# Expert outputs weighed and added in pieces of 128 rows, in a one-core language-model layer

## The reference

```
h = emb[tokens] * sqrt(256) + pos_enc            # 256 wide
h = softmax(q k^T / 16, over queries) v          # q, k, v = h w_q, h w_k, h w_v
h = h + mixer(layernorm(h))                      # projection, causal convolution over 4 steps,
                                                 # state-space scan in chunks of 128, gate, norm, projection
# mixture of 8 experts, two per token, 1024 slots each
scores = softmax(layernorm(h) @ w_router);  weights, experts = top_k(scores, 2)
slot   = expert * 1024 + position of this choice among the expert's choices
y      = gelu(x[slots of e] @ w1[e]) @ w2[e]     # 256 -> 1024 -> 256, for each expert e
out    = h + sum over a token's two experts of weight * y + bias
```

## Time and profile before

| | us |
|---|---|
| median of 3 runs (957.86 to 961.7) | 959.34 |
| the profiled execution, its own time | 958.16 |
| its span | 956.4 |
| mean granted TensorE clock | 0.965 of full speed |
| PE busy | 887.6 (93% of the span) |
| DVE, ACT, POOL busy | 631.6, 529.1, 505.9 |
| batches: from the start to the last scatter | about 559 |
| experts: from there to the end | about 397 |

### The profile page before, as it was taken

One profiled execution on the slowest core, in us unless ns is written; L12 is line 12 of the kernel. 1 busy time (PEld: TensorE's weight loads), 2 busy tenths in 40 slices (PEclk: granted clock), 3 DMA queues, 4 the chain that ended last, 5 costly groups with the idle time before them and its releaser, 6 DMA issues.

```text
span 956.4 us, 17255 instructions
## 1 busy us (share of the span) xinstructions
PE 887.6 (93%) x5580; PEld 785.6 (82%) x5580; DVE 631.6 (66%) x1662; ACT 529.1 (55%) x1094; POOL 505.9 (53%) x503
## 2 busy tenths in 40 slices
PE   5799999999999999999998539999999999999994
PEld 3688888888888888888886429999999999999993
DVE  2477899888988898889887344646363636363631
ACT  1466776677667767776766134545444544444430
POOL 6257776787678767877788311232333232323342
PEclk8799999999999999999998759999999999999998
DMA  8900011001000000000000034343343433332120
GB/s 269 330 26 12 34 46 33 22 33 33 12 22 13 23 13 23 20 16 14 21 22 26 14 103 132 90 88 105 67 109 72 109 72 104 72 105 28 23 61 34
DMA packets 48653, 58.62 MB, mean 61 GB/s; under 512 B 6336, under 2 KB 43819, under 8 KB 48624
## 3 DMA queue, kind: packets, MB, share of 16 engines
q1 hardware_dynamic: 33552, 41.05, 13.1%
q0 software_dynamic: 13632, 17.02, 10.6%
q10 hardware_dynamic: 1440, 0.17, 0.1%
HBM read 34.14 MB, written 29.75 MB: 67 GB/s over the span
## 4 chain that ended last, share of the span: by engine, by line
PE 81%; DVE 10%; issue 3%; POOL 2%; DMA 2%; ACT 1%; DVEq 0%; POOLq 0%; SPq 0%
PE bank L1592 13%; PE bank L1593 13%; PE bank L1594 13%; PE bank L1387 11%; PE bank L1497 5%; PE bank L1332 4%; PE bank L1477 4%; PE bank L1371 3%; PE bank L1346 3%; PE bank L1362 3%; PE bank L1353 3%; PE bank L1449 2%; DVE seg L1051 2%; PE bank L1512 2%; PE bank L1604 2%
## 5 line engine op out<-in xcount | busy, mean ns | idle before, releaser
L637 POOL DMA_INDIRECT out<-ye,tok_slot x56 | 96.7, 1727 | 254.3 <-DMA out<-ye,tok_slot 138.0
L877 ACT ACTIVATE hf<-bank 128x512 f32<-128x512 f32 x128 | 79.5, 621 | 202.4 <-PE bank L1594 201.1
L1264 DVE TENSOR_TENSOR h_lo<-hf,h_hi 128x512 fp32r<-128x512 f32 x128 | 88.6, 693 | 99.9 <-ACT h_hi L879 99.9
L1592 PE MATMUL bank<-w_hi,h_hi 128*128 128x256 f32 x512 | 146.2, 286 | 0.0
L1593 PE MATMUL bank<-w_lo,h_hi 128*128 128x256 f32 x512 | 144.9, 283 | 0.0
L1594 PE MATMUL bank<-w_hi,h_lo 128*128 128x256 f32 x512 | 144.9, 283 | 0.0
L1023 DVE SCALAR_TENSOR_TENSOR xc<-bank,cw,xc 128x253 f32<-128x253 f32 (+2 forms) x288 | 128.2, 469 | 1.7
L1592 PE MATMUL bank<-xe_hi,w_hi 128*128 128x512 f32 x256 | 100.8, 394 | 2.7 <-DVE xe_lo L1256 2.7
L1593 PE MATMUL bank<-xe_lo,w_hi 128*128 128x512 f32 x256 | 100.4, 392 | 0.0
L1594 PE MATMUL bank<-xe_hi,w_lo 128*128 128x512 f32 x256 | 100.2, 391 | 0.0
L585 POOL DMA_INDIRECT slots_dram<-rows,slot x64 | 63.4, 991 | 67.8 <-DVE slot L1152 53.2
(11 more groups left out here) (203 smaller groups left out, 2311.2 us busy)
## 6 DMA issues: line engine op xcount, KB each, us to landing
w_raw<-w SPq DMA_DIRECT2D x16, 1024.0 KB
slots_dram<-zero_row SPq DMA_DIRECT2D x1, 8320.0 KB, 29.7
xe<-slots_dram SPq DMA_DIRECT2D x16, 520.0 KB, 4.4
out<-hb SPq DMA_DIRECT2D x16, 256.0 KB, 2.1
w_raw<-in_wT SPq DMA_DIRECT2D x1, 1288.0 KB, 9.1
slots_dram<-rows,slot POOLq DMA_INDIRECT x64
out<-ye,tok_slot POOLq DMA_INDIRECT x64, 3.7
xg<-emb,idx POOLq DMA_INDIRECT x36, 4.1
```

The source lines that it names most:

```text
L637: g.indirect_dma_start(out, bass.IndirectOffsetOnAxis(ap=tok_slot[q][:, j:j + 1], axis=0), ye[q][:, j, :], None, compute_op=ALU.add).then_ ...
L877: sc.activation(hf[m % 2][:, :], h_bank[i % H_BANKS][:, :], ACT.Gelu_apprx_tanh)\
L1264: vc.tensor_tensor(h_lo[:, m, :], hf[m % 2][:, :], h_hi[:, m, :].bitcast(F32), ALU.subtract)\
L1592: te.matmul(out_, hi, rhi, start=first_, stop=False)
```

## The change

Three edits that have nothing to do with each other.

1. `second_product` alternates its four products between the two banks, one product of 128x256 in a bank at a time (`y_bank[j % 2]`), and waits on `ye_ready` before each. DVE weighs each product by itself (`tensor_scalar`, 128x256), and signals each; POOL waits for each piece. `low_weights` stays ahead of the first and the third weighing. The last group uses the same two banks; `last_product`, `weigh_onto` and `LAST_BANKS` go. Of the last expert only pieces 4 to 7 are fetched into `base` and written plainly; pieces 0 to 3 are added with accumulation as for other experts, after POOL has waited for the four fetches.
2. In the drain step that has b but no f, `gated_root` stands ahead of `scatter_rows`. In all other steps the order is as before.
3. SP waits for `w_q` and `w_k` to land before it issues `w_v`, `w_in` and `w_out`.

```diff
+            sp.wait_ge(s_qk, 32)
             sp.dma_start(wv[:, :, :], w_v.rearrange("(k p) n -> p k n", p=P)).then_inc(s_early, 16)
...
                 if t:
                     describe_rows(t, p)
+                if b and not f:
+                    gated_root(b, q)
+                if t:
                     scatter_rows(t, p)
-                if b:
+                if b and f:
                     gated_root(b, q)
...
             def fetch_sums():
 
-                for j in range(JS):
-                    g.indirect_dma_start(base[:, j, :], None, out,
+                for j in range(JS // 2, JS):
+                    g.indirect_dma_start(base[:, j - JS // 2, :], None, out,
...
+                pool.wait_ge(fetched, 16 * (JS // 2))
 
             def write_sums():
 
-                for j in range(JS):
+                for j in range(JS // 2):
+                    add_rows(NE, 1, j)
+                for j in range(JS // 2, JS):
...
                 def weigh(g):
                     q, half = g // NG, g % NG
-                    for b in range(2):
-                        if half == NG - 1 and not (last and q):
-                            low_weights(r * 2 + q, 1 - q, b, (w1_split, w2_split)[b])
-                        j = 4 * half + 2 * b
-                        dve.wait_ge(y_psum, r * (4 * NG) + (Y0 + 2 * g + b + 1 - 4 * NG))
-                        vc.tensor_tensor(ye[q][:, j:j + 2, :], y_bank[b][:, :].rearrange("p (j d) -> p j d", j=2),
...
+                    for n in range(4):
+                        if half == NG - 1 and n % 2 == 0 and not (last and q):
+                            low_weights(r * 2 + q, 1 - q, n // 2, (w1_split, w2_split)[n // 2])
+                        j = 4 * half + n
...
+                        dve.wait_ge(y_psum, r * (2 * JS) + (Y0 + 4 * g + n + 1 - 2 * JS))
...
+                            ins = vc.tensor_scalar(ye[q][:, j, :], y_bank[n % 2][:, 0:DM], w_slot[q][:, j:j + 1], None,
+                                                   ALU.mult)
+                        ins.then_inc(ye_ready, 1)
...
                 def second_product(g):
-                    q = g // NG
-                    pe.wait_ge(w2_split, r * 2 + (q - 1))
-                    for b in range(2):
-                        pe.wait_ge(ye_ready, r * (4 * NG) + (2 * g + b + 1 - 4 * NG))
-                        for j in (2 * b, 2 * b + 1):
-                            dst = y_bank[b][:, (j % 2) * DM:(j % 2 + 1) * DM]
...
+                    q = g // NG
+                    pe.wait_ge(w2_split, r * 2 + (q - 1))
                     for j in range(4):
...
+                        pe.wait_ge(ye_ready, r * (2 * JS) + (4 * g + j + 1 - 2 * JS))
```

More of the change, by code:

```diff
@@ L272, in lm_block @@
         ye = [eb(f"ye{q}", [P, JS, DM]) for q in range(2)]
-        base = eb("base", [P, JS, DM])
+        base = eb("base", [P, JS // 2, DM])
         e_now = eb("e_now", [P, 1])
@@ L360, in lm_block @@
         expert_added = sem("expert_added")
-        H_BANKS, Y0, CHUNKS = 4, 4 * NG, KF
+        H_BANKS, Y0, CHUNKS = 4, 2 * JS, KF
         CHUNK = 2 * KD * FF // CHUNKS
@@ L1265, in split_h @@
                             .then_inc(hlo_ready, 1)
-                def weigh_onto(g):
-                    half = g % NG
-                    if half == 0:
-                        dve.wait_ge(fetched, 16 * JS)
-                    for j in range(4 * half, 4 * half + 4):
-                        if half == 0:
-                            row, at = y_bank[j // 2], (j % 2) * DM
-                            dve.wait_ge(y_psum, Y0 + 4 * NG * (NE // 2 - 1) + 2 * g + j // 2 + 1)
-                        else:
-                            row, at = LAST_BANKS[j - 4], 0
-                            dve.wait_ge(y_psum, Y0 + 4 * NG * (NE // 2 - 1) + 2 * g + j - 4 + 1)
-                        ins = vc.scalar_tensor_tensor(out=ye[1][:, j, :], in0=row[:, at:at + DM],
-                                                      scalar=w_slot[1][:, j:j + 1], in1=base[:, j, :],
-                                                      op0=ALU.mult, op1=ALU.add)
-                        if half or j % 2:
-                            ins.then_inc(ye_ready, 1)
@@ L1285, in weigh @@
                 def weigh(g):
                     q, half = g // NG, g % NG
-                    for b in range(2):
-                        if half == NG - 1 and not (last and q):
-                            low_weights(r * 2 + q, 1 - q, b, (w1_split, w2_split)[b])
-                        j = 4 * half + 2 * b
-                        dve.wait_ge(y_psum, r * (4 * NG) + (Y0 + 2 * g + b + 1 - 4 * NG))
-                        vc.tensor_tensor(ye[q][:, j:j + 2, :], y_bank[b][:, :].rearrange("p (j d) -> p j d", j=2),
-                                         bc(w_slot[q][:, j:j + 2].unsqueeze(2), [P, 2, DM]), ALU.mult)\
-                            .then_inc(ye_ready, 1)
+                    for n in range(4):
+                        if half == NG - 1 and n % 2 == 0 and not (last and q):
+                            low_weights(r * 2 + q, 1 - q, n // 2, (w1_split, w2_split)[n // 2])
+                        j = 4 * half + n
+                        if last and g == 2 * NG - 1 and n == 0:
+                            dve.wait_ge(fetched, 16 * (JS // 2))
+                        dve.wait_ge(y_psum, r * (2 * JS) + (Y0 + 4 * g + n + 1 - 2 * JS))
+                        if last and g == 2 * NG - 1:
+                            ins = vc.scalar_tensor_tensor(out=ye[q][:, j, :], in0=y_bank[n % 2][:, 0:DM],
+                                                          scalar=w_slot[q][:, j:j + 1], in1=base[:, n, :],
+                                                          op0=ALU.mult, op1=ALU.add)
+                        else:
+                            ins = vc.tensor_scalar(ye[q][:, j, :], y_bank[n % 2][:, 0:DM], w_slot[q][:, j:j + 1], None,
+                                                   ALU.mult)
+                        ins.then_inc(ye_ready, 1)
@@ L1304, in experts @@
                         split_x(g + 1)
-                    if last and g >= NG:
-                        weigh_onto(g)
-                    else:
-                        weigh(g)
+                    weigh(g)
                     if g + 1 == NG:
@@ L1629, in last_product @@
                             at = slice(m * DM, (m + 1) * DM)
[L1630 to L1631 removed]
+                            ins = three(y_bank[j % 2][:, 0:DM], h_hi[:, m, j * P:(j + 1) * P],
+                                        h_lo[:, m, j * P:(j + 1) * P], w_hi[q][:, 1, at], w_lo[q][:, 1, at],
                                         m == 0, m == KF - 1)
[L1633 to L1647 removed]
                         ins.then_inc(y_psum, 1)
@@ L1656, in experts @@
                         turn_x(g + 1)
-                    if last and g + 1 == 2 * NG:
-                        last_product(g)
-                    else:
-                        second_product(g)
+                    second_product(g)
             experts(1, None)
```

28 lines of the change are left out of this document (8 added, 20 removed).

## The result

The changed kernel takes 968.93 us (median of 4 runs, 967.17 to 971.28); the kernel before took 958.6 beside it (4 runs, 957.26 to 961.7). The ratio is 1.0109, with a 95% interval of 1.0081 to 1.0137: some 10.3 us slower. The forecast was 963.8 with a range of 960.5 to 967.5. The direction was right, and the size was half of what came; the time lies above the range. The profiled execution is the one of 971.28, with a span of 969.5 us.

A forecast was written before the change was run, and what follows sets the result against it. PE was taken as the bound, with 81% of the chain. Stalls 8.4, end -0.75, drain +0.3 and start -2.7 gave +5.25 on 958.16, or 963.4; forecast 963.8, between that and the runs' median, range 960.5 to 967.5.

The forecast's parts named there:

- The stalls: Experts' groups with a weight split: PE waits 1.4 us for product 0's weighing, 7 times; 6 shift POOL's end, +8.4 us.
- Edit 2, +0.3: Drain step: the root runs earlier, but the later scatters delay the second root L558; +0.3 us, bounds -0.15 and +0.7.
- Edit 3, -2.7: Start: 2 MB of loads no longer compete with PE's two gathers; -2.7 us, bounds -3.3 and -1.2.
- Rival (a): Start: edit 3 gives nothing because late w_v or w_in makes POOL or DVE the wait; 966.1 us, chance 0.12.
- The estimate of 2.3 us: Start: a 128 KB gather would take 2.3 us by the skill's fit, so edit 3 would bring 3.5; outside the sum.
- The end, -0.75: POOL's last stretch: holds, fewer fetches, shorter wait and adds for writes sum to -0.75 us, bounds -1.8 and +0.5.
- the four adds: Last expert's end on POOL: four adds replace four writes, 18.6 us for 13.97, +4.6.
- from the first fetch to the first add: Last expert's end on POOL: four fetches instead of eight, -5.0 us, and a shorter wait behind the last fetch, -1.1.
- the holds and the later split: POOL before the last fetches: own holds for pieces 5 and 7 and a later weight split, +0.75 us, from none to 1.
- rival (c): Experts: the TensorE clock falls in the stalls, one slow product each, 17.3 us more; 980.7 us, chance 0.04.

The follow-up runs named there:

- edit 1 alone: Kernel before with only the 128-row products and weighings and the last expert's first half added: 968.55 us, ratio 1.0106.
- gathers_first: Kernel before, with the loads of in_wT and out_wT waiting until the first two gathers have landed, w_v issued as before: 960.6 us, ratio 1.0003.
- edit 3 alone: Kernel before with only SP's wait for the query and key weights ahead of the value weights and the loads behind them: 960.45 us, ratio 1.0016.
- the new end alone: Kernel before with only the last expert's end changed to four fetches, four adds and four writes: 958.16 us, ratio 0.9986.
- late splits: Changed kernel, all three edits, with the two weight splits moved behind the weighings of products 0 and 2: 957.07 us, ratio 0.9981.
- both splits ahead: Changed kernel with both weight splits ahead of the first weighing: 993.6 us, one run.
- bias_late: Changed kernel with the small load bias_b issued only once the first two gathers have landed: 968.68 us, one run.
- edit 2: As a run: kernel before with only the gated root moved ahead of the scatters in the drain step: 959.95 us, ratio 1.0010.
- late splits in the kernel before: Kernel before, banks of two products, with only the two weight splits moved behind the weighing of their bank: 960.41 us, ratio 1.0012.
- edit 1 with late splits: Kernel before with edit 1 and the two weight splits behind the weighings of products 0 and 2, no other edit: 956.0 us, ratio 0.9964.

## Why the forecast was half right

By its own steps:

- **The stalls, 7 waits and 6 in POOL's frame, 8.4 us: right in mechanism, place, number and size.** 1.45 each for a forecast of 1.4, and 8.48 in POOL's frame in the changed kernel, 8.13 in edit 1 alone. Moving the split away took them away, and doubling it ahead of the weighing gave 3.4 for 1.2. The weighing took 0.48 us and not 0.41, inside its bounds. No stall in the groups without a split: right.
- **Edit 2, +0.3: right.** L558 is released by a scatter, and the gain of the earlier root is taken back: -0.08 in the trace, +0.3 by the medians, neither to be told from nothing.
- **Edit 3, -2.7 (bounds -3.3 and -1.2): this is the step that failed**, in the sentence "2 MB of loads no longer compete with the two gathers that PE waits for". They do compete: the wait ends at 5.19, the gather was issued at 5.47 and needs about 4 us to land, as the 3.9 from its issue to PE's start in `gathers_first` and the median of 4.1 say, so the loads flow again before it has its bytes, and from 8 to 10 us not one byte of it moves in the changed kernel (in the profile of edit 3 alone the gathers' queue moved 0.04 MB there). Edit 3 alone cost 1.4 us in place of giving 2.7, a miss of 4.1 us, most of the 5.1 between forecast and result. Rival (a) was nearest (966.1), but it stopped at a gain of nothing. The estimate of 2.3 us that the forecast worked out beside the sum, by the fit in the Trainium skill (DMA: Bandwidth & Descriptors, Anatomy of one DMA — SWDGE (gpsimd) path), was of the same kind: it priced a gather with the engines to itself, and the shortest landing in the earlier trace rows is 3.4. That a gather takes its turn beside the loads, packet by packet (the Trainium skill, DMA: Bandwidth & Descriptors, Queues, rings and completion order), isn't what the changed kernel's trace shows from 8 to 10 us, where the gathers' queue has no packet at all and the two others have 320; why, no run shows. I had priced what a load removed gives, where the change only delays it; the gain was there for the taking only when the loads waited for the gathers' landing, and then POOL bounded it to 1.0.
- **The end, -0.75 (bounds -1.8 and +0.5): too low.** It was +0.89 in the changed kernel, +0.33 in edit 1 alone, +0.22 with the new end alone. The mis-sized term is the four adds: 18.6 forecast, from one add cycle of 4.71; they took 20.24, 19.79 and 19.87, since one of the four cycles is 5.4 to 6.0 us long; why wasn't found. The other terms were right: from the first fetch to the first add 7.43 in place of 13.37, -5.9 for a forecast of -6.1, and the holds and the later split ahead of the fetches 20.34 in place of 19.85, +0.5 for a forecast of +0.75. Of that 0.39 is the longer hold of the add of piece 4 under the weight split (3.21 for 2.82, last section).
- **The clock, rival (c): rightly set aside**, for a stall of this length.

The sum with what was measured: 8.5 + 0.3 to 0.9 + 0 + 1.4 = 10.2 to 10.8, for 10.3 by the medians. The 1.4 of edit 3 is the loosest of these terms: its interval runs from 0.1 to 2.9 us.

**What stays open.** In the profiles the experts' first product starts between 567.80 and 572.16. Set against the first root (L522 at the start), the fourteen starts sort themselves. In twelve profiles the experts start 540.1 to 540.8 us behind that root, whatever the edits; their whole spread was there at the start, where the root runs at 27.10 to 30.59. Only the changed kernel (544.44) and `gathers_first` (543.73) have some 3.5 us more, and these are the two in which the granted clock stays at 0.50 from 526 us to 538 and later; in the others it is back by 532 at the latest. `gathers_first` was 1.68 us ahead of the kernel before at its last root of the loop (489.92 against 491.60) and 1.96 behind at the experts' start. The 3.6 us of the drain in the changed kernel's profiled execution are no fixed price of its edits: the versions with late splits and with both splits ahead and `bias_late` have the same drain code and stand at 540.10, 540.55 and 540.23. What decides when the clock comes back was not found.

## What to carry to other kernels

When buffers are halved, look at what stands ahead of their reader on its engine: a piece of work that was hidden beside the second half of the old buffer lies on the path once the writer waits for the first half. Put it behind the short instruction that frees the buffer, and the smaller pieces gain (here -3.65 us in place of +9.5). And a load that is delayed isn't a load that is removed: ask whether it is still held when the transfer that it disturbs needs its bytes, and who waits for the delayed load next.

## What the runs showed of the hardware

- **How long a standstill costs the clock.** Behind the 7 stalls of 1.20 us in the changed kernel, and the 14 in edit 1 alone and `bias_late`, the granted clock stayed at 1.00. Of 7 stalls of 3.41 us it fell to 0.50 at six, at a price of 1.4 to 2.7 us each, which is up to 80% of the stall again. At the start, a wait of 3.46 us for the gather is followed by eight matmuls in 3.75, and a wait of 0.42 us by the same eight in 1.96.
- **The length of the slow stretch isn't the kernel's.** With one and the same code at the start, the second group of eight matmuls there took 1.99 us in four profiles (before, edit 1, edit 2, late splits in the kernel before) and 3.78 in two (the new end, edit 1 with late splits), 1.8 us of difference. The Trainium skill (TensorE: Matmul & The Clock Gate, What's actually happening) says that the number of slow matmuls at a start varies from run to run of one kernel; the traces agree. A comparison of single executions is blind to 2 us for this alone, and to 3.6 more for the drain step.
- **The clock's row isn't complete.** In the profile of edit 3 alone the granted clock reads 1.00 in all windows from 12 to 24 us, while eight matmuls take 3.75 and 3.78 there. The durations tell, not the row.
- **An add under a weight split waits for its end.** POOL's indirect add mostly holds its engine for 1.54 us. Where it starts while DVE's weight split runs, it ends 1.41 to 1.46 us after the split does, however much of the split was left, in all 96 such adds of thirteen profiles: 2.82 us for a start 0.88 into the split (892.40 before), 3.21 for one 0.49 into it (905.13). So it is as if the issue began when the split ends. In the version with both splits ahead no add starts under a split, and the adds of piece 4 take 1.54.
